# Score maxima and neighbour maxima in one part, second experts' outputs in other PSUM banks, and graph 0 joined first

## What is computed

```python
x = x + gnn0(adj, layernorm(x))     # max over the first 25 neighbours, concat, 256 -> 128, relu
x = x + ffn0(layernorm(x))          # 8 experts 128 -> 512 -> 128 (gelu), top 2 of a router
x = x + attention(layernorm(x), adj)  # 8 heads of 16, masked by adj, Wo, bo
x = x + ffn1(layernorm(x))          # 6 experts 128 -> 128 -> 128 -> 128 (relu), top 2 of a router
```

## Time and profile before

| | us |
|---|---|
| median of three runs | 3596.99 |
| lowest and highest | 3594.17, 3603.11 |
| profiled execution | 3601.75 |
| its span | 3599.6 |
| PE, DVE, ACT, POOL busy | 2146.0, 1776.8, 1226.7, 1106.3 |
| granted PE clock, mean | 0.803 of full speed |

### The profile page before, as it was taken

One profiled execution on the slowest core, in us unless ns is written; L12 is line 12 of the kernel. 1 busy time (PEld: TensorE's weight loads), 2 busy tenths in 40 slices (PEclk: granted clock), 3 DMA queues, 4 the chain that ended last, 5 costly groups with the idle time before them and its releaser, 6 DMA issues.

```text
span 3599.6 us, 46254 instructions
## 1 busy us (share of the span) xinstructions
PE 2146.0 (60%) x14209; PEld 1346.9 (37%) x14209; DVE 1776.8 (49%) x5239; ACT 1226.7 (34%) x2295; POOL 1106.3 (31%) x1215
## 2 busy tenths in 40 slices
PE   0010332057847775686748684677658778785687
PEld 0010231044425532454435442454345435442344
DVE  4134127167626663666446662566446436525713
ACT  2001122024623353235513462235423443362153
POOL 3536455431642144303540254313440110100000
PEclk9985675577968887797959896788869888897898
DMA  4323754662474236623564247523663044203000
GB/s 114 39 45 72 139 120 105 95 150 85 92 130 110 92 69 91 155 91 71 98 129 122 66 85 124 112 84 70 102 134 109 21 74 151 75 24 53 25 7 7
DMA packets 190672, 318.14 MB, mean 88 GB/s; under 512 B 28975, under 2 KB 115244, under 8 KB 190380
## 3 DMA queue, kind: packets, MB, share of 16 engines
q1 hardware_dynamic: 156844, 245.99, 24.3%
q0 software_dynamic: 33536, 68.75, 16.5%
HBM read 271.31 MB, written 42.93 MB: 87 GB/s over the span
## 4 chain that ended last, share of the span: by engine, by line
issue 35%; DVE 27%; PE 26%; DVEq 5%; ACT 4%; DMA 2%; SPq 1%; ACTq 0%
DVE parts L1221 7%; PE PA L1579 4%; PE PA L1582 4%; PE PY L1594 4%; ACT HB L1375 2%; PE PH L1529 2%; DVEq L861 2%; DVE res_f L1115 2%; PE PA L1556 2%; PE PY L1541 2%; DVE score L909 1%; DVE top L913 1%; PE PH L1636 1%; DMA rows_cols<-sorted_x 1%; DVE st L870 1%
## 5 line engine op out<-in xcount | busy, mean ns | idle before, releaser
L1221 DVE CUSTOM_DVE_ANT_0 parts<-PA,mask 128x1024 bf16<-128x1024 f32 x512 | 625.5, 1222 | 291.6 <-issue 291.6
L803 POOL DMA_INDIRECT G<-table,slot_idx x512 | 526.7, 1029 | 270.2 <-issue 270.2
L1375 ACT ACTIVATE HB<-PA 128x1024 f32<-128x1024 f32 x512 | 498.9, 1020 | 323.4 <-PE PA L1582 321.2
L1556 PE MATMUL PA<-KS,QS 96*128 96x512 bf16 x1024 | 356.2, 441 | 261.5 <-DVE res_f L1115 141.5
L1579 PE MATMUL PA<-QS,KS 99*128 99x512 bf16 x1024 | 420.6, 411 | 102.2 <-ACT HB L1375 69.9
L636 POOL TENSOR_TENSOR pool_pad<-pool_pad 1x1 f32<-1x1 f32 x146 | 29.1, 200 | 1462.0 <-DMA sorted_y<-rows_y 743.2
L1582 PE MATMUL PA<-identb,mask 128*128 128x128 bf16 x4096 | 423.8, 229 | 0.0
L639 DVE MEMSET dve_pad<- 1x1 f32 x699 | 41.1, 59 | 751.9 <-DMA G_more<-table,slot_idx 434.5
L1582 PEld LDWEIGHTS PA<-identb,mask 128*128 128x128 bf16 x4096 | 338.8, 103 | 141.1 <-issue 31.5
L803 POOL DMA_INDIRECT G_more<-table,slot_idx x280 | 287.1, 1025 | 173.4 <-issue 173.4
L1358 ACT ACTIVATE HB<-PH,block_b 128x128 f32<-128x128 f32 x736 | 209.6, 368 | 353.7 <-PE PH L1529 353.6
(11 more groups left out here) (218 smaller groups left out, 3291.1 us busy)
## 6 DMA issues: line engine op xcount, KB each, us to landing
wbuf<-in_L_ffn_W SPq DMA_DIRECT2D x128, 512.0 KB, 4.2
adj_sb<-in_adj SPq DMA_DIRECT2D x64, 512.0 KB
adjm<-in_adj SPq DMA_DIRECT2D x64, 512.0 KB
HB<-in_L_ffn_W SPq DMA_DIRECT2D x32, 512.0 KB, 3.6
parts<-in_L_ffn_W SPq DMA_DIRECT2D x24, 512.0 KB, 4.8
parts_dram<-parts SPq DMA_DIRECT2D x16, 768.0 KB, 4.0
QS<-parts_dram SPq DMA_DIRECT2D x48, 256.0 KB, 9.3
KS<-parts_dram SPq DMA_DIRECT2D x48, 256.0 KB, 19.5
```

Source lines behind the costliest of these rows:

```text
L803: pool.indirect_dma_start(G[:, t % 2, s, :] if s < few else G_more[:, s - few, :], None, table, bass.IndirectOffsetOnAxis(slot_idx[:, t, s ...
L1221: ins = dve.tensor_tensor_reduce(out=junk, in0=psum(ps, step)[:, :], in1=mask[:, t, :], scale=1.0, scalar=LOWEST, op0=ALU.add, op1=ALU.max ...
L1375: act.activation(HB[:, kc % 2, 2 * pr:2 * pr + 2, :], psum(ps, key)[:, :].rearrange("p (h q) -> p h q", h=2), ACT.Exp, scale=float(D) ** - ...
L1556: ins = pe.matmul(psum(ps, step)[:, half[hf]], QS[0:SROWS, h, t * P:(t + 1) * P], KS[0:SROWS, h, half[hf]], start=True, stop=True)
```

## The change

- Groups of block outputs have two blocks instead of four (`Y_GROUP`, 12 groups instead of 6); the sorted rows still come four blocks at a time.
- `FETCHED` goes from 4 to 2, so `POOLED` from 3 to 1: the second part of a pass fetches tiles 0 and 1 and takes the maximum of tile 0 only, due at 105; the first part of the next pass does the other seven maxima, 16 units apart.
- `y1` uses the ring PY instead of PA.
- In the pass that has first experts but no attention (pass -1), the block outputs are fetched and joined, and q, k, the stacks and v are made, before the remaining gathers and maxima of graph 1.
- `shift` stands at the end of the first part; its place among the neighbouring steps is the same in the other passes.

```diff
+Y_GROUP = 2
+Y_GROUPS = (BLOCKS + Y_GROUP - 1) // Y_GROUP
-FETCHED = 4
+FETCHED = 2
 def group_of(j):
-    g = j // PER_GROUP
-    return g, j == min(BLOCKS, (g + 1) * PER_GROUP) - 1
+    g = j // Y_GROUP
+    return g, j == min(BLOCKS, (g + 1) * Y_GROUP) - 1
...
+    rest = []
     if near:
-        streams.append([(15.0 * (t - POOLED), ("pmax", t), (("fetch", t),)) for t in range(POOLED, TILES)])
-        streams.append([(15.0 * (t - POOLED) - 14.0, ("fetch", t), (("pmax", t - 1),)) for t in range(FETCHED, TILES)])
+        rest.append([(16.0 * (t - POOLED) + 1.0, ("pmax", t), (("fetch", t),)) for t in range(POOLED, TILES)])
+        rest.append([(16.0 * (t - POOLED) - 14.0, ("fetch", t), (("pmax", t - 1),)) for t in range(FETCHED, TILES)])
+    if att or not unit:
+        streams += rest
...
-    s = merge([k for k in streams if k], held)
-    streams = [[(0.0, ("shift",), ())]]
+    s = merge([k for k in streams if k], held) + [("shift",)]
+    streams = []
...
-    if unit:
+    if unit and att:
         streams.append([(2.0, ("fetch_y",), ())])
...
+    elif unit:
+        s += [("fetch_y",), ("comb",), ("lnv", 2), ("ln", 2), ("qT",), ("qk", 0), ("qk", 1), ("next_mask",),
+              ("stack",), ("v",)] + merge(rest, held)
...
-        streams.append([(30.0 + 15.0 * t, ("fetch", t), (("find", t), ("store_x",), ("pmax", t - 1)))
+        streams.append([(30.0 + 35.0 * t, ("fetch", t), (("find", t), ("store_x",), ("pmax", t - 1)))
                         for t in range(FETCHED)])
-        streams.append([(82.0 + 17.0 * t, ("pmax", t), (("fetch", t),)) for t in range(POOLED)])
+        streams.append([(105.0 + 17.0 * t, ("pmax", t), (("fetch", t),)) for t in range(POOLED)])
...
     if k == "y1":
-        return A(*step)
+        return Y(*step)
```

More of the change, by code:

```diff
@@ L698, in body @@
                         sp.wait_ge(*is_taken(ps, turn, ("y", g)))
-                        n = min(PER_GROUP, BLOCKS - g * PER_GROUP)
-                        sp.dma_start(sorted_yv[:, g * PER_GROUP:g * PER_GROUP + n, :],
+                        n = min(Y_GROUP, BLOCKS - g * Y_GROUP)
+                        sp.dma_start(sorted_yv[:, g * Y_GROUP:g * Y_GROUP + n, :],
                                      rows_y[:, g % 2, 0:n * C].rearrange("p (q c) -> p q c", c=C)
@@ L844, in body @@
                         for i in range(2):
-                            g = GROUPS - 2 + i
+                            g = Y_GROUPS - 2 + i
                             pool.wait_ge(*at(ps, turn, f"yst{g % 2}", ("yst", g)))
@@ L1249, in body @@
                         if (qh, g) == (0, 0) and ps.unit:
-                            for i in (GROUPS - 2, GROUPS - 1):
+                            for i in (Y_GROUPS - 2, Y_GROUPS - 1):
                                 dve.wait_ge(*at(ps, turn, f"yst{i % 2}", ("yst", i)))
@@ L1363, in body @@
                         g = step[1]
-                        n = min(PER_GROUP, BLOCKS - g * PER_GROUP) * C
+                        n = min(Y_GROUP, BLOCKS - g * Y_GROUP) * C
                         act.wait_ge(*is_full(ps, turn, ("y", g)))
@@ L1535, in body @@
                         g, last = group_of(j)
-                        q = j % PER_GROUP
+                        q = j % Y_GROUP
                         pe.wait_ge(*is_taken(ps, turn, ("up", j)))
```

## The result

The changed kernel takes 3426.84 us (median, 3424.31 to 3432.26); the kernel before takes 3595.58 beside it. The ratio is 0.9534, interval 0.9508 to 0.9559: 169 us less. The profiled execution spans 3430.5 us against 3599.6, at a mean granted clock of 0.814 against 0.803. The forecast was 3414.

The account below looks back on a forecast made before the run. No engine was full: POOL's gather chain bounds second parts, PE and DVE handing two banks back and forth first parts. Terms sum to -182.6 us from 3601.75, giving 3419.2, or 3414 on the median's footing; range 3345 to 3530.

Parts of the forecast that it names:

- (a): Second parts of passes 0 to 4: without maxima 1 and 2, PE's wait ahead of fin goes, 130.6 us gained.
- what is late next is PE itself: Second parts of passes 0 to 4: once the stall ahead of fin goes, PE comes next; tile 0's gathers are long in.
- (b): First parts of passes 4 and 5: DVE's waits at tile 3's maximum go, 50 us gained.
- (c): First parts of passes 1 to 7: y1 in PY ends score products' waits on acc1, 114.5 us gained; bounds 0 and 141.5.
- (e): First parts of passes 1 to 5: two more maxima make PE wait while both PA banks are full, 24 us lost.
- (f): Pass starts 1 to 5: stacks delay sorted rows, 27.5 us lost (bounds 0, 10 each), and tile 2's maximum, 15 us lost.
- R1: Rival: the wait moves to PY, where a block group's first dn needs a bank acc1 must free; 3529 us, chance 0.13.
- (d): Block groups of two: six more ACT copies and SP stores per pass, taken as nothing; 17 us without cover.
- R2: Rival: stacks and tiles 1 and 2 collide at pass boundaries, costing 125 us against 42.5 booked; 3497 us, chance 0.19.
- R4: Rival: gathers bound the starts of first parts, exposing 51 us a pass in five passes; 3654 us, chance 0.06.
- (g): Pass -1 to the end of pass 0's first part: POOL waits for the blocks and join, 46 us lost; bounds 10 and 90.
- The 4 us a pass start: Pass starts: 0.5 MB of gathers sharing DMA queue rows would lengthen the stacks' flight by about a sixth, some 4 us.

Follow-up runs that it names:

- the PY edits alone: Kernel before with only block groups of two and y1 in PY; gathers, maxima and pass -1 as before: 3452.22 us, ratio 0.9605.
- the gathers moved alone: Kernel before with FETCHED at 2 and the new due times; y1 in PA, groups of four, head as before: 3499.37 us, ratio 0.9726.
- an eighth of the stacks: Changed kernel loading one of eight heads of QS and KS in passes with attention: 3362.16 us, ratio 0.9347; on the slower chip 3714.78 us.
- the one with the early maximum: Changed kernel with pass -1 ordered as before and tile 0's maximum due at 84 instead of 105: 3350.01 us, ratio 0.9319.
- the head as before: Changed kernel with pass -1 ordered as before, graph 1's gathers beside graph 0's blocks: 3718.69 us, ratio 0.9588, on the slower chip.

## Why the prediction was right in the total and less so in its terms

The total was 13 us off, with the mechanism as forecast, but three terms were missed by some 20 us or more each and a fourth by 17. That they cancelled is luck.

(a) **Second parts.** The waits of the earlier trace rows went entirely, and PE waits for nothing ahead of fin. Yet the second parts gave 114 us, not 130.6, and take 163 to 180 us where 165 to 172 were forecast. What took the difference is DVE's start of passes 2, 3 and 4: 11.96, 12.24 and 12.17 us by "issue" instead of 4.42, 4.25 and 4.52, 23 us in three passes. My step that "what is late next is PE itself" overlooked it. The old stall had kept the stacks out of the jump's way: with the PY edits alone, where the stall stays, these pauses are 4.1 to 4.5 us, with the gathers moved alone 11.0 to 12.1, and with an eighth of the stacks 6.3 to 7.4.

(b) **Tile 3.** DVE's waits at tile 3 in passes 4 and 5 are gone (0.7 us in pass 4). Those parts fell from 219 and 205 to 191 and 187 us, their share of (c) included. With the gathers moved alone they took 205 and 206: most of the 50 us gained there was spent again by (e) and (f).

(c) **y1 in PY.** Booked 114.5. With groups of two and nothing else it gives 144 us, taken out of the changed kernel it costs 133. The waits on acc1 went as expected and did not move to PY (0.4 us in pass 3): R1 fell. Two sizes were off. The waits for MX that come in exchange are 56 us, not 27. And PE's busy time falls, a term that was not in the sum at all. With the PY edits alone it falls by 58 us in first parts 1 to 7, and 141.5 - 55.7 + 58 = 144, near the 153 us by which these parts are shorter. Two executions of the changed kernel differ by 25 us in PE's busy time (2099.5 and 2074.2), so this term's size is known to some 20 us only.

(d) **Groups of two.** Taken as nothing, and no run has this edit alone. The nearest pair is the gathers moved alone (groups of four) and the changed kernel with y1 in PA (groups of two), which differ in the head besides: with groups of two first parts 1 to 7 are 9 us longer (1379 against 1370) and second parts 0 to 4 are 6 shorter (855 against 861). So the cost is small beside the 17 us allowed without cover, and not told apart from nothing. Pass 7 has no first experts and so says nothing of groups; its first part is shorter by 17 us with (c), booked at 20, and 14 us longer with y1 back in PA.

(e), (f) **Seven maxima and the stacks in first parts.** Booked 24 + 27.5 + 15 = 66.5 less the 50 of (b), 16.5 net. The gathers moved alone lengthen first parts by 48, the same edits on top of the PY edits by 76 (1245 against 1169). So this term was mis-sized by 30 to 60 us. Its parts, in the kernel with the gathers moved alone: waits for MX grew by 68 against 39 booked (24 + 15), those for sorted rows by 61 against 27.5, some 12 us a pass in passes 1 to 5 where my upper bound was 10. The price of "up to 2.4 us each" for a wait on MX was wrong where DVE itself stands at a maximum: the longest in pass 3 is now 14.6 us. R2 was thus nearer than its chance of 0.19 said. The smaller stacks show what traffic costs, in this and in (a): 65 us. DVE waits at tile 2 for 10.5, 9.4 and 12.4 us in passes 1 to 3, inside the bounds of (f) but partly over the 0 to 10 given as a sign; R4, which needed 37 us a pass beyond it, fell.

(g) **The head.** Booked 46 lost; 22 were. The whole difference arises in pass -1, up to the join. Its blocks run from 339 to 402, not to 419, POOL fetches their outputs by 426, not 447, and the join's work on DVE is done at 457, not 490. From there on the forecast holds: the last maximum ends 125 us later (forecast 123), pass 0 begins at 677 instead of 703 (700 in the kernel before), and its first part takes 198 us where the forecast has 196. So the blocks (63 us, not 73), the fetch and the join were priced too high. What the sum did not look at is that the old head gains from the other edits: the gathers moved alone end pass 0's first part 32 us earlier than before. Against that kernel the joined head costs 54 us, against the one with the early maximum 59.

The 4 us a pass start that I had estimated from the sharing of queue rows in the Trainium skill (DMA: Bandwidth & Descriptors, Queues, rings and completion order) are not tested: they price gathers beside the stacks, and no run takes the gathers away. The run with smaller stacks takes the stacks away and shows another price, 6 us at DVE's start and 10 on the rows in pass 3.

Sum as measured: -114 - 77 + 22 = -169. The forecast of the same three groups: -130.6, then -50 - 114.5 + 24 + 27.5 + 15 = -98, then +46.

## What to carry to other kernels

When PE's short waits are counted, count what they do to its clock too: the same instructions took 8% longer in the stage with the waits, and PE's busy time made up a third or more of what moving y1 gave. A stall that is removed may have been keeping a burst of transfers away from the next stage's start; look for what waits by "issue" or for small loads right behind such a burst. And an edit that comes bundled with good ones (here the joined head, 54 to 59 us) is found only by taking it out alone.

## What the hardware showed that I had not expected

**A loop's jump is slow beside a burst of transfers.** At the starts of passes 2, 3 and 4, where the program jumps back, the first instructions of DVE, ACT and POOL were late together. At pass 2's start in the changed kernel (ACT, then POOL):

```profile
1404.49 1.28 ACT L1319 ACT_TABLE_LOAD   x1 [11.07 <-issue]
...
1400.99 0.18 POOL L644 TENSOR_TENSOR pool_pad<-pool_pad 1x1 f32<-1x1 f32 x1 [5.54 <-issue]
```

DVE's pause was 4.3 to 4.5 us in the kernel before, whose stacks had landed by then, 12 in the changed one, and 6.3 to 7.4 with an eighth of their bytes (3.1 to 3.4 on the slower chip). Passes 1, 5 and 6 begin with the same work and no jump, and DVE has no such pause there. The trace has a DMA kind of its own for instructions. In DVE's pause at pass 2's start, from 1396 to 1408.2 us, it shows (packets, MB, share):

```profile
q14 instruction: 3, 0.02, 1.4%
q8 instruction: 1, 0.02, 0.7%
```

The Trainium skill (Runtime: NRT & Kernel Launch, Instruction fetch mechanics) says that a taken branch out of the fetched pages makes a DMA fetch of the target before the engine goes on. The trace agrees: in the 30 us from the pause's start 9 packets of q14 and 2 of q8 are moved, in the 30 us from the starts of passes 1, 5 and 6, without a jump, 3, 1 and none of q14 and none of q8. That these packets come late because of the stacks is read from the kernels compared under (a) above; no run shows one packet waiting behind another, and why the smaller stacks leave 6 to 7 us on one kind of chip and 3 on the other is open.

**Chips differ by 8% for the same kernel.** On the slower ones second parts, with their gathers, are some 50 to 63 us longer (238 against 175 us for pass 1, in the kernels with the head as before), while pass 6's is the same 131 us, and ACT and DVE wait by "remote", a releaser that no trace of the other kind shows; the longest, with y1 in PA on the slower chip:

```profile
1838.07 0.21 ACT L1353 ACTIVATE ed<-dlt 128x8 f32<-128x8 f32 x1 [24.52 <-remote]
```

What causes it is open.
